# The last batch on its way from attention to experts: norms and PSUM copies on ScalarE, block by block, and a projection fused in pairs of heads

## What is computed

```
x = x + layernorm(attn(layernorm(x)))
x = x + layernorm(moe(layernorm(x)))

# attn: q, k projected by Wq, Wk and then by Wproj to one number a token and head
z_k, z_q = (k @ Wproj.T), (q @ Wproj.T)
ctx[i] = sum_j max(0, 1 - |z_q[i] - z_k[j]| / bandwidth_h) * v[j] / T

# moe: top 8 of 64 experts, capacity 128, each silu(gate) * up, then down;
# beside them one shared expert of width 512 with a sigmoid gate
```

## Time and profile before

| | |
|---|---|
| time, median of 3 runs | 2455.28 us (2450.02 to 2457.62) |
| the profiled execution's own time | 2456.26 us |
| its span in the profile | 2455.0 us |
| granted TensorE clock, mean | 0.906 |
| busy share of PE, DVE, ACT, POOL | 80%, 82%, 78%, 41% |

### The profile page before, as it was taken

The page is one execution under the profiler, slowest core; times in us unless marked ns, Lnnn a source line. Parts: engine busy times, 40 slices in busy tenths (PEclk is TensorE's granted clock), DMA queues, the critical chain, the costliest instruction groups (busy, mean ns, idle before and its releaser), DMA issues.

```text
span 2455.0 us, 30185 instructions
## 1 busy us (share of the span) xinstructions
PE 1961.3 (80%) x11666; PEld 779.4 (32%) x11666; DVE 2015.5 (82%) x2895; ACT 1923.6 (78%) x1242; POOL 999.9 (41%) x356
## 2 busy tenths in 40 slices
PE   7788889789669889886788889778898884899920
PEld 4433233233112223221222322112232333677720
DVE  5497888797999998999998989998999986644348
ACT  2398998898999999999999999999999970122223
POOL 1020110100335367364284466342574371276754
PEclk9899999899889999998999999888999995788965
DMA  6315244335120212131202030312111018478779
GB/s 220 131 61 197 84 156 149 122 106 201 57 103 11 88 31 82 41 110 43 95 31 80 20 107 20 123 49 83 50 58 56 20 46 222 108 188 185 179 197 314
DMA packets 182039, 259.26 MB, mean 106 GB/s; under 512 B 22280, under 2 KB 162184, under 8 KB 173704
## 3 DMA queue, kind: packets, MB, share of 16 engines
q1 hardware_dynamic: 167408, 237.83, 29.1%
q0 software_dynamic: 12288, 18.88, 4.5%
q10 hardware_dynamic: 2200, 0.60, 0.1%
HBM read 187.25 MB, written 70.03 MB: 105 GB/s over the span
## 4 chain that ended last, share of the span: by engine, by line
PE 35%; ACT 28%; DVE 24%; POOL 5%; issue 4%; DMA 3%; SPq 1%; DVEq 0%; POOLq 0%; ACTq 0%
ACT TB L1036 28%; PE ps L860 11%; DVE TB L1348 9%; PE ps L766 5%; PE ps L804 4%; DVE TB L1372 4%; PE ps L811 3%; DVE st L1084 2%; PE ps L953 2%; POOL scr L1514 2%; DVE TB L1346 2%; POOL rs L1506 1%; POOL ve L1504 1%; PE ps L914 1%; PE ps L832 1%
## 5 line engine op out<-in xcount | busy, mean ns | idle before, releaser
L1036 ACT ACTIVATE TB<-ZB,nzk 128x2048 f32<-128x2048 f32 x938 | 1794.7, 1994 | 144.4 <-PE ps L860 97.6
L860 PE MATMUL ps<-TB,V 128*32 128x512 f32 x8192 | 1106.0, 641 | 275.6 <-DVE TB L1348 260.0
L1348 DVE TENSOR_SCALAR TB<-TB 128x2048 f32<-128x2048 f32 x938 | 1129.0, 1228 | 101.0 <-ACT TB L1036 98.9
L860 PEld LDWEIGHTS ps<-TB,V 128*32 128x32 f32 x8192 | 208.8, 113 | 1002.8 <-DVE TB L1348 625.0
L1514 POOL TENSOR_TENSOR scr<-ebase,scr 128x256 f32<-128x256 f32 x12 | 509.7, 42471 | 0.0
L1504 POOL TENSOR_SCALAR ve<-mv 128x4 f32<-128x4 f32 x64 | 84.1, 1314 | 837.0 <-DVE mv L1088 837.0
L804 PE MATMUL ps<-XF,wsgu 128*128 128x512 f32 x512 | 259.1, 631 | 1.1 <-DVE TB L1255 0.6
L1372 DVE SCALAR_TENSOR_TENSOR TB<-ZB,kz 128x2048 f32<-128x2048 f32 x86 | 212.2, 2468 | 4.2 <-PE ps L860 4.2
L1512 POOL TENSOR_TENSOR scr<-ebase,scr 128x4 f32<-128x4 f32 x12 | 29.4, 2452 | 388.1 <-DVE scr L1209 388.1
L1063 ACT ACTIVATE ZB<-ps 128x128 f32<-128x128 f32 x64 | 17.7, 277 | 189.7 <-PE ps L953 189.7
L804 PEld LDWEIGHTS ps<-XF,wsgu 128*128 128x128 f32 x512 | 92.2, 197 | 149.3 <-issue 141.9
(11 more groups left out here) (178 smaller groups left out, 1639.2 us busy)
## 6 DMA issues: line engine op xcount, KB each, us to landing
ZB<-zq_rows SPq DMA_DIRECT2D x64, 1024.0 KB, 7.3
scr<-fused_w SPq DMA_DIRECT2D x48, 512.0 KB, 3.5
TB<-in_egu_w SPq DMA_DIRECT2D x44, 256.0 KB, 3.5
y_rows<-zero SPq DMA_DIRECT2D x20, 512.0 KB, 5.1
fused_w<-TB SPq DMA_DIRECT2D x4, 2048.0 KB, 6.7
TB<-y_rows SPq DMA_DIRECT2D x16, 512.0 KB, 8.5
XF<-in_x SPq DMA_DIRECT2D x24, 256.0 KB, 3.2
v_rows<-scr SPq DMA_DIRECT2D x24, 256.0 KB, 2.1
```

Source lines behind the costliest of these rows:

```text
L860: ins = pe.matmul(ps[c][32 * j:32 * j + 32, :], V[:, o:o + 32], tile(t)[:, 512 * c:512 * c + 512], start=(kb == 0), stop=(kb == KB - 1))
L1036: act.activation(tile(e), zrow(head), ACT.Abs, bias=nzk[b][:, kb * H + g:kb * H + g + 1], scale=1.0).then_inc(s_abs, 1)
L1348: dve.tensor_scalar(T, T, 1.0, 1.0, ALU.min, ALU.subtract).then_inc(s_bump, 1)
```

## The change

Front: the 32 fused matmuls are cut otherwise. `("M", p, hh, cc, j)` takes rows and columns 32j to 32j+31 (two heads) of all 16 blocks: 32 rows deep instead of 128, and still 512 columns. Four that follow each other use four different strips of rows and four banks. ScalarE copies j = 0, 1, 2 (24 copies) and VectorE j = 3 (8 copies). SyncE writes the fused weights after all 32, in the same four DMAs.

Last batch: ScalarE copies the four result banks (`qc`) into four buffers, the transposes go to banks 4 to 7, and `cn`, `hn` and both halves of the copy after h's transposes (`hT2`) are ScalarE's. GpSimd gives it scale and bias (`pool_affine`, four small instructions in place of two). VectorE keeps moments, the sum x1 (`xs`) and the router, block by block. x of the last batch is loaded at slot 206 of its attention, into two row buffers that are free by then. The nine x1 loads for the end move from `sync_tail`'s start to the expert loop, one for every four experts. TensorE's order takes logits, half of the shared expert's first block and counts of each block together; its down part stands after `pv`. `vector_slots` for the two halves of group 0 stay ahead of the first expert, those of group 1 move to step 0 of the loop, and a gather waits only for its own half.

```diff
 def fused_units():
-    return [("M", p, hh, cc, tq) for tq in range(4) for p in range(2) for hh in range(2) for cc in range(2)]
+    return [("M", p, hh, cc, j) for p in range(2) for hh in range(2) for cc in range(2) for j in range(4)]
...
-            pe.matmul(ps[k][:, :], wqk[p][:, hh, 128 * cc:128 * cc + 128], BD[:, 4 * tq:4 * tq + 4, :],
+            r = slice(32 * j, 32 * j + 32)
+            pe.matmul(ps[k][:, :], wqk[p][r, hh, 128 * cc:128 * cc + 128], BD[r, :, 32 * j:32 * j + 32],
...
+    if b == NB - 1:
+        sy += [(206 + 2 * k, "a", b, k) for k in range(4)]
...
 def tail_first():
-    o = [("hT", b, 0, 0), ("hT", b, 0, 1), ("hT", b, 1, 0), ("hT", b, 1, 1), ("lg", b, 0)]
-    o += [("hT", b, 2, 0), ("hT", b, 2, 1), ("lg", b, 1), ("hT", b, 3, 0), ("hT", b, 3, 1), ("lg", b, 2), ("lg", b, 3)]
-    g = gate_units(b, 0)
-    o += g[0:4] + [("mT", b, 0)] + g[4:6] + [("mT", b, 1)] + g[6:8] + [("mT", b, 2)]
-    return o + [("mT", b, 3), ("dn", b, 0, 0), ("dn", b, 0, 1)]
+    o = hT[0] + [lg[0], up[0]] + hT[1] + [lg[1], up[1]] + hT[2] + [lg[2], mT[0]] + hT[3] + [lg[3], up[2], mT[1], up[3]]
+    return o + [mT[2], gate[0], mT[3]] + gate[1:4]
...
+            elif what == "qc":
+                act.activation(cT4[k], ps[bank][:, :], ACT.Copy).then_inc(empty[bank], 1)
+            elif what in ("cn", "hn"):
+                act.wait_ge(s_crs if what == "cn" else s_xrs, 4 * b + k + 1)
+                for i in range(4):
+                    ins = act.activation(dst[i], src[i], ACT.Identity, bias=nb[k][:, i:i + 1], scale=rs[k][:, i:i + 1])
+                ins.then_inc(s_cn if what == "cn" else s_h, 1)
+            elif what == "hT2":
+                for c in range(2):
+                    act.activation(hT_of(b, k)[:, c, :], ps[bank][:, :], ACT.Copy).then_inc(empty[bank], 1)
...
         def scalar_tail():
             for k in range(4):
-                scalar_stage("hT", b, k)
+                scalar_stage("qc", b, k)
+            for k in range(3):
+                scalar_stage("cn", b, k)
+            scalar_stage("hn", b, 0)
+            scalar_stage("cn", b, 3)
+            scalar_stage("hT2", b, 0)
+            for k in range(1, 4):
+                scalar_stage("hn", b, k)
+                scalar_stage("hT2", b, k)
             for k in range(4):
                 scalar_stage("ex", b, k)
+            for m in range(4):
+                scalar_stage("gu", b, 0, m)
...
         def vector_tail(v):
-            for k in range(4):
+            for k in range(3):
+                vector_quad_scale(15, k)
                 vector_both(v, "cst", b, k)
+            vector_stage(v, "xs", b, 0)
+            vector_both(v, "xst", b, 0)
+            vector_quad_scale(15, 3)
+            vector_both(v, "cst", b, 3)
+            for k in range(1, 4):
+                vector_stage(v, "xs", b, k)
+                vector_both(v, "xst", b, k)
             for k in range(4):
+                vector_stage(v, "lg", b, k)
                 vector_stage(v, "rm", b, k)
                 vector_stage(v, "re", b, k)
                 if k:
+                    vector_stage(v, "sc", b, k - 1)
+            vector_stage(v, "sm", b, 0)
+            vector_stage(v, "sm", b, 1)
             vector_stage(v, "sc", b, 3)
...
+        def pool_affine(s, moments, n, done, p, eps=1e-5):
+            pool.wait_ge(moments, n)
+            pool.tensor_scalar(nb[s][:, :], view(mv[s][:, 0, 0:1], 0, [[2, 4]]), -1.0, None, ALU.mult)
+            pool.tensor_scalar(ve[s][:, :], view(mv[s][:, 0, 1:2], 0, [[2, 4]]), eps, None, ALU.add).then_inc(s_p, 1)
+            pool.wait_ge(s_p, p.up())
+            pool.tensor_tensor(rs[s][:, :], ve[s][:, :], mhalf[:, 0:4], ALU.pow).then_inc(s_p, 1)
+            pool.wait_ge(s_p, p.up())
+            pool.tensor_tensor(nb[s][:, :], nb[s][:, :], rs[s][:, :], ALU.mult).then_inc(done, 1)
...
         def tensor_tail():
-            tensor_slots(0)
-            tensor_slots(1)
+            tensor_stage("dn", last, 0, 0)
+            tensor_slots(0, 0)
+            tensor_slots(0, 1)
+            tensor_stage("dn", last, 0, 1)
...
+            for n in range(NW, NE):
+                sync_expert(n)
+                if n % 4 == 2 and n // 4 - 4 in range(NX1):
+                    sync_x1(n // 4 - 4, q_px)
...
-            pool.wait_ge(s_idx, 2 * (n // 8) + 2)
+            pool.wait_ge(s_idx, 2 * (n // 8) + 1 + n % 8 // 4)
```

More of the change, by code:

```diff
@@ L141, in bank_uses @@
             take(("q", q, nn), nn)
-        for t in range(4):
+        for t in range(4 if q < 15 else 0):
             take(("qt", q, t), 7)
@@ L150, in bank_uses @@
             ring += 1
-    for unit in tail_order():
-        take(unit, 4 + ring % 3)
-        ring += 1
-    take(("pv",), 7)
+    for t in range(4):
+        take(("qt", 15, t), 4 + t)
+    for unit, k in tail_first() + tail_middle():
+        take(unit, k)
+    for i, unit in enumerate(tail_order()):
+        take(unit, 4 + i % 3)
     for g in range(8):
@@ L205, in slots_in_step @@
 def slots_in_step(n):
+    if n == 0:
+        return 1
     if n % 8 == 3 and n // 8 + 2 < 8:
@@ L292, in build @@
         mv = [sb(f"mv{i}", [128, 4, 2]) for i in range(5)]
+        nb = [sb(f"nb{i}", [128, 4]) for i in range(4)]
         ve = [sb(f"ve{i}", [128, 4]) for i in range(5)]
@@ L360, in fused_piece @@
         def fused_piece(unit):
-            _, p, hh, cc, tq = unit
-            return view(T0, 4096 * tq + 512 * cc + 256 * p + 128 * hh, [[1024, 4], [1, 128]])
+            _, p, hh, cc, j = unit
+            return view(T0, 512 * cc + 256 * p + 128 * hh + 32 * j, [[1024, 16], [1, 32]])
         def mbuf(t):
@@ L540, in sync_program @@
             sp.dma_start(Y[0][TOK:TOK + 128, :], zero[:, 0:C]).then_inc(q_zero, 16)
+            for unit in fused_units():
+                k, m = use[unit]
+                sp.wait_ge(empty[k], m + 1)
             for tq in range(4):
-                for unit in fused_units()[8 * tq:8 * tq + 8]:
-                    k, m = use[unit]
-                    sp.wait_ge(empty[k], m + 1)
                 sp.dma_start(MD[4 * tq:4 * tq + 4].rearrange("t p c -> p t c"),
@@ L596, in sync_stage @@
                 if b == last:
-                    sp.wait_ge(*tile_used(1023))
+                    for o in (NB * H - 6, NB * H - 5):
+                        for w in row_used(o):
+                            sp.wait_ge(*w)
                 elif k > 1:
@@ L616, in sync_stage @@
                 sp.wait_ge(s_xs, 4 * b + k + 1)
[L617 removed]
+                sp.dma_start(X1v[4 * b + k], x1_of(b, k) if b == last else x_of(b, k)).then_inc(q_x1[k], 16)
             elif what == "h":
@@ L692, in sync_tail @@
             for k in range(4):
+                sp.wait_ge(q_x1[k], 64)
+                sp.wait_ge(q_h[k], 64)
+                for c in range(2):
+                    kk, mm = use["hT", b, k, c]
+                    sp.wait_ge(full[kk], mm + 1)
+            for n in range(6, 8):
+                sync_expert(n)
+            for k in range(4):
                 sp.wait_ge(q_w2[k], 64)
@@ L1146, in vector_stage @@
             elif what == "cst":
-                bank, u = use["qt", 4 * b + 3, 3]
+                bank, u = use["qt", 4 * b + 3, k if b == last else 3]
                 dve.wait_ge(empty[bank], u + 1)
@@ L1153, in vector_stage @@
                 vector_norm(k, rows4(c4), rows4(c4), s_cn, i)
-                if b == last and i:
-                    dve.wait_ge(s_cn, 4 * b + k + 1)
-                    dve.wait_ge(q_a[k], 16 * (b + 1))
-                    dve.tensor_tensor(x_of(b, k), x_of(b, k), c4, ALU.subtract).then_inc(s_xs, 1)
+            elif what == "xs":
+                if k == 0:
+                    dve.wait_ge(*tile_used(1023))
+                dve.wait_ge(s_cn, 4 * b + k + 1)
+                dve.wait_ge(q_a[k], 16 * (b + 1))
+                dve.tensor_tensor(x1_of(b, k), x_of(b, k), ctxn[:, 4 * k:4 * k + 4, :], ALU.subtract).then_inc(s_xs, 1)
             elif what == "xst":
@@ L1180, in vector_stage @@
                 dve.wait_ge(full[bank], u + 1)
+                if b == last and k == 0:
+                    dve.wait_ge(q_y, 192)
                 if b == k == 0:
@@ L1350, in vector_program @@
                     vector_stage(v, *e)
-            for step in range(6):
-                vector_quad_out(15, step)
             vector_tail(v)
@@ new lines, in vector_hits @@
+        def vector_hits(c, i, v):
+            sl = slice(8 * c + 4 * i, 8 * c + 4 * i + 4)
+            s4 = view(iof, 0, [[0, 4], [1, 128]])
+            end = view(CS[:, sl, 127:128], 0, [[128, 4], [0, 128]])
+            dve.tensor_tensor(hit[:, sl, :], s4, view(prev_c, 8 * c + 4 * i, [[1, 4], [0, 128]]), ALU.is_ge)
+            dve.wait_ge(s_hit, 2 * c + i)
+            dve.tensor_tensor(t2_, s4, end, ALU.is_lt).then_inc(s_v, 1)
+            dve.wait_ge(s_v, v.up())
+            dve.tensor_tensor(hit[:, sl, :], hit[:, sl, :], t2_, ALU.mult).then_inc(s_hit, 1)
@@ L1442, in vector_tail @@
```

(2 more changed lines are left out.)

218 lines of the change are left out of this document (103 added, 115 removed).

## The result

The changed kernel took 2411.79 us (median of 4 runs, 2407.97 to 2415.98) against 2452.99 us for the kernel before in the same measurement: a ratio of 0.983, 95% interval 0.981 to 0.985. Timed once more beside two experiments it gave 0.984 (0.981 to 0.987). The forecast was 2420 with a range of 2405 to 2436, so the direction and the range held, and the median is 8 us lower than the likeliest case (2.3 of these are the kernel before, whose median here is 2452.99 where the forecast had 2455.28). The profiled execution after has a span of 2414.7 us against 2455.0, so 40.3 us less.

The account below looks back on a forecast made before the run. No engine was taken to bound the kernel throughout, so each stage was read by itself. Terms -11 - 17.5 - 8.6 + 0 + 2 = -35.1 against 2456.3 gave 2421.2, the median 1.0 below: 2420, range 2405 to 2436.

Parts of the forecast that it names:

- likeliest case: Whole kernel: the single most likely time, 2420 us, with 0.52 chance of landing within 10 us of it.
- Front: Fusing the weights: four row strips side by side, z starting at 40 us, 11 us less, bounds 0 and 14.
- 37 for full clock and 42 for half: Front: expected z start in us, 37 if TensorE has its full clock there, 42 at half; 40 was taken.
- The rival that strips don't overlap: Front: row strips don't run side by side and TensorE's 27.5 us stand: 2431, chance 0.10.
- Last tile to last logits: Last batch after attention: last logits at 2060.5 in place of 2077.9, 17.5 us less, bounds 11 and 24.
- The middle between half and full: Last batch's three later blocks: 9.6 us each at half clock, 5.2 at full; last logits taken midway, 2060.5.
- Last logits to last count: Last batch: one search left after the last logits, not four; 10.5 us for 19.1, 8.6 less, bounds 5.6 and 9.6.
- DRAM trip: Counts' way through DRAM after the last count: stays at 10.5 us, fewer transfers in flight left out.
- Counts to first expert: Last count to first expert: removed index work and added down part give 0, bounds 4 less and 4 more.
- Expert loop: 36 experts: nine x1 loads bring DMA share from 0.86 to 0.97, 2 us more, bounds 0 and 14.
- Slower rival (scatters' chain): Expert loop: x1 loads raise scatter landing to about 7.7 us, so that chain sets the loop: 2464, chance 0.03.
- early front given back: Attention: the time gained by the earlier front is lost again there: 2431, chance 0.03.

Follow-up runs that it names:

- the second experiment: The changed kernel with the 32 fused units ordered so that eight in a row use the same strip of 32 rows: 2451.74 us, ratio 0.9995.
- counts-first: Changed kernel with all logits first, masks as early as possible, block 3's count before weight sums; x1 loads among or ahead of experts: 2413.70 and 2412.57 us.

## Why the prediction was right, point by point

**Front, 11 less: 10.7.** The mechanism held: the strips ran side by side, as the second experiment shows. But that the size is met so closely in this trace is luck: its clock rose last of all. The sum had 37 for full clock and 42 for half; over eleven traces with this front z began between 35.5 and 40.1, in six of them at 36.0 or before. Against the one trace of before that is at least 14.8 us less, beyond the bound of 14: at full clock the 3 us put on for mutual waits were too much. What the full gain depends on, when the clock rises, was in the forecast only as the step from 37 to 42. Single numbers were off. Eight instructions of four strips take 1.4 to 1.5 us at the full clock, not "about 1", because ScalarE's three copies for each such group of four units are 3 x 0.525 us (12.6 / 24) = 1.58; that the copies would set the pace was in the forecast. Until the banks are full it is quicker: single records of the last group (33.76) show four strips starting within 20 ns, and eight instructions in 0.96 us. The writes ended long before zq, as forecast. The Trainium skill ("TensorE: Matmul & The Clock Gate", Part 3) gives 3.07 times for four row tiles; the trace bears out the overlap, and as copies hold it after the first eight instructions it can't confirm the factor. The same page (Why this matters for your kernels) says that a single short matmul takes as long as a deep one. The traces agree at the same clock: 1056 ns for 32 rows and 1057 for 128 at half, 587 and 592 at full. But the short ones by themselves stayed at 1.2 GHz for 56 us.

**The rival that strips don't overlap** was priced at 2431 with TensorE's old 27.5 us. The second experiment shows that the price was too low: without overlap the clock stays down too, z begins at 77.8, and the whole gain is gone at 2451.74. I had not seen that the two go together.

**Last tile to last logits, 17.5 less: 19.2.** The way to the first transposes was nearly exact: TensorE began them 15.0 us after the last tile, where the sum had 14.3. In it the ScalarE norm was mis-sized, 2.07 us against 1.7 (an instruction of L1075, with one pointer operand, takes about 493 ns by the trace, and one of the norm, with two, 586 to 590). The Trainium skill ("ScalarE: Activation LUTs", What ACT_TABLE_LOAD costs) had it: 93 ns more for each pointer operand, which makes 0.37 us more a norm, an estimate by which it is 2.1; the trace agrees. Against it stood the clock. The middle between half and full was taken; in the changed kernel it rose during the first up unit, so three blocks took 17.8 us together, 5.9 each, near the lower end of 5.2 to 9.6. One wait was missing: the copy after the first transposes stands behind the context norm of block 3, which costs 1.4 us. The engine for the norms matters little: 0.6 us at the first logits, and 2 to 3 at the last, most of it by what the clock did. The rest is the order by block with ScalarE's PSUM copies. Of these two the order has the larger part: eight copies of 0.69 us left VectorE, 5.5 us at most, an estimate from its durations before. And a clock up from the first block on isn't needed: the two counts-first traces, at the half clock up to the third block's logits and without the up half between, have 41.1 us too. In the forecast's reading of before, 70 instructions at 0.50 should be 96 (32 transposes and 64 of the logits); nothing hangs on it.

**Last logits to last count, 8.6 less: 7.8.** Right in size, the reason only in part. The sum has TensorE's three 512-column units set when the last mask comes; in the trace that mask waits for VectorE's search. VectorE's count and two sums of weights behind it, which the sum also has, hold the last count for another 3.1 us. Counts first takes 4.2 us off, 2.4 of it by VectorE's order.

**DRAM trip, 0: 2.0 less.** The step "fewer transfers are in flight, which I leave out" was the wrong one. Putting the nine loads back brings the trip from 9.8 (10.4 in the second trace of the changed kernel) to 11.6 us. That is what moving them is worth, and it is little: in the whole time no run shows it (2410.51 us with them back).

**Counts to first expert, 0: 1.4 more.** Within its bounds. Neither attempt to better it won anything: with the down part earlier the indices lost the clock, and with the indices later the gathers waited in the loop.

**Expert loop, 2 more: 3.5 less.** The step failed in sign. The loads cost the loop nothing that these traces show (0.2 us between two traces of equal clock). The DMA share was to go from 0.86 to 0.97; over the loop it went from 0.75 to 0.77, with 193 GB/s in place of 169. TensorE's clock, which I had not among the terms of this stretch, goes with 5 us between the traces with the new tail (214.3 at 0.95 to 219.3 at 0.92). Nearly all of the 5 us between the forecast's sum and the profiled span is this one term; the rest cancels: logits 1.7 less and trip 2.0 less than forecast, front 0.3, attention 0.4, counts 0.8, first expert 1.4 and the end 1.0 more. That the sum comes so near is in part luck, since terms of 2 to 5 us missed on both sides.

**Slower rival (scatters' chain), early front given back:** neither happened. Scatters held GpSimd up for 10.6 us in all over the loop, in 8 waits of at most 1.6 us, and attention took 1926.9 us against 1926.5.

## What to carry to other kernels

A stage in which engines take turns is worth reordering by block before its arithmetic is spread over more engines: the order, with the PSUM copies on ScalarE, gave 17 us here, and the second engine for the norms 2, most of which was the clock as well. When short matmuls are cut by rows, the four strips must alternate instruction by instruction; in the other order this kernel lost all that the whole change gives, since the clock didn't rise. And before a few us in a stretch bound by TensorE are put down to an edit, read the granted clock of that stretch in both traces: here 0.91 to 0.95 went with 5 to 6 us, more than most of the edits.

## What the runs showed of the hardware that I had not expected

- TensorE busy without a gap with matmuls 32 rows deep, one strip at a time, stayed at 1056 ns an instruction for 56 us (64 instructions, 16.5 to 72.5). The 128-row transposes and matmuls behind them stayed at the half clock for 5 us more, until 77.8, and then had 0.45 us an instruction. With the four strips in turn the clock was up 4 to 17 us after the first of them, in all eleven traces.
- The same instruction order reached the full clock at different times from one execution to the next: in the front between 20.2 and 32.9 us over eleven traces, and in the last batch 10 us after the first transposes in one kernel and 23 us in two others whose order up to there is the same.
- Attention, unchanged in all, took between 1921.3 and 1928.8 us over thirteen traces. What sets this was not looked into.
- Why the expert loop gets 0.91 of the clock in one execution and 0.95 in another stays open: no experiment controlled it.
